# Second layer norm of a gated attention from the first one's variance, both inverse roots in one GpSimd operation

## The reference, cut to what matters

```python
def _layernorm(x, axis=-1, eps=1e-05):
    m, v = jnp.mean(x, axis=axis, keepdims=True), jnp.var(x, axis=axis, keepdims=True)
    return (x - m) / jnp.sqrt(v + eps)

x = x + _L0_ffn_ref(_layernorm(x), ...)        # sublayer 4: gate, top 2 of 8 experts, shared expert
x = x + _L1_attn_a_ref(_layernorm(x), ...)     # sublayer 5: the gated attention

def _L1_attn_a_ref(x, ...):                    # its x is already a layer norm
    residual = x
    mu, var = jnp.mean(x, -1, keepdims=True), jnp.var(x, -1, keepdims=True)
    xn = (x - mu) / jnp.sqrt(var + 1e-5) * gamma + beta
    ...                                        # q, k, v, alpha from xn; a scan over time
    return out + residual
```

## Time and profile before

| | us |
|---|---|
| runs (3) | 1042.56, 1044.42, 1044.64; median 1044.42 |
| the profiled execution, its own time | 1036.55 |
| its span, first to last instruction | 1034.8 |
| mean granted TensorE clock, share of full | 0.937 |

### The profile page before, as it was taken

The page is one execution under the profiler, slowest core; times in us unless marked ns, Lnnn a source line. Parts: engine busy times, 40 slices in busy tenths (PEclk is TensorE's granted clock), DMA queues, the critical chain, the costliest instruction groups (busy, mean ns, idle before and its releaser), DMA issues.

```text
span 1034.8 us, 16383 instructions
## 1 busy us (share of the span) xinstructions
PE 906.0 (88%) x5966; PEld 514.3 (50%) x5988; DVE 787.1 (76%) x1853; ACT 414.9 (40%) x686; POOL 369.4 (36%) x460
## 2 busy tenths in 40 slices
PE   8899999999999898879989875799999878988786
PEld 3344444444433465554434342565667456766454
DVE  5578888767788677788767679747666998788985
ACT  2445565554433354333534356123222334331233
POOL 6282333223343453422444320323021344343433
PEclk9899999999999988889999987899999899998889
DMA  5363122202000000000000000000000000000000
GB/s 130 97 177 103 48 69 62 73 1 108 0 1 1 1 2 1 1 1 2 0 1 1 1 0 2 2 1 1 1 2 1 1 1 1 2 1 3 1 10 31
DMA packets 11531, 24.32 MB, mean 24 GB/s; under 512 B 1323, under 2 KB 7635, under 8 KB 11315
## 3 DMA queue, kind: packets, MB, share of 16 engines
q1 hardware_dynamic: 11152, 22.30, 7.4%
q10 hardware_dynamic: 294, 0.91, 0.3%
HBM read 15.69 MB, written 7.34 MB: 22 GB/s over the span
## 4 chain that ended last, share of the span: by engine, by line
PE 57%; DVE 32%; issue 4%; POOL 3%; ACT 2%; DMA 0%; DVEq 0%; POOLq 0%; ACTq 0%
PE ps L1082 4%; PE ps L1075 4%; PE ps L1069 4%; PE ps L419 4%; PE ps L369 3%; DVE a_MN L549 2%; PE ps L2166 2%; DVE XN L166 2%; PE ps L389 2%; PE ps L2163 2%; DVE g_C L1922 2%; PE ps L2769 2%; DVE r_PP L2818 2%; PE ps L2177 1%; PE ps L1051 1%
## 5 line engine op out<-in xcount | busy, mean ns | idle before, releaser
L1322 POOL TENSOR_TENSOR f_Y<-f_Y,f_TT 128x512 f32<-128x512 f32 x54 | 69.9, 1294 | 126.9 <-DVE f_TT L1168 126.8
L549 DVE TENSOR_REDUCE a_MN<-ps 128x1 f32<-128x384 f32 (+3 forms) x154 | 93.1, 637 | 25.1 <-PE ps L372 23.4
L119 POOL TENSOR_TENSOR rs<-t,mhalf 128x4 f32<-128x4 f32 x36 | 37.4, 1038 | 131.5 <-DVE t L102 130.3
L673 ACT ACTIVATE a_PT<-ps 128x1024 f32<-128x1024 f32 x56 | 57.4, 1025 | 58.3 <-PE ps L389 58.1
L1082 PE MATMUL ps<-f_HH,pack_zero 128*128 128x512 f32 x128 | 67.7, 611 | 10.1 <-DVE f_TT L1168 10.1
L1268 ACT ACTIVATE f_HH<-ps,pack_zero 128x512 f32<-128x512 f32 x64 | 44.0, 687 | 71.1 <-PE ps L1069 71.1
L1069 PE MATMUL ps<-f_XS,pack_zero 128*128 128x512 f32 x128 | 67.6, 610 | 1.4 <-DVE f_XS L1037 0.9
L1075 PE MATMUL ps<-f_XS,pack_zero 128*128 128x512 f32 x128 | 68.7, 619 | 0.0
L1168 DVE SCALAR_TENSOR_TENSOR f_TT<-ps,pack_zero,f_X 128x512 f32<-128x512 f32 x64 | 47.7, 745 | 27.5 <-PE ps L1082 26.7
L369 PE MATMUL ps<-a_KS,a_QS 72*128 72x128 bf16 (+3 forms) x224 | 53.8, 303 | 8.2 <-DVE a_MN L549 7.2
L769 POOL TENSOR_SCALAR_AFFINE_SELECT a_PT<-a_PT 128x256 f32<-128x256 f32 x64 | 26.2, 413 | 87.8 <-ACT a_PT L673 87.2
(11 more groups left out here) (342 smaller groups left out, 2191.8 us busy)
## 6 DMA issues: line engine op xcount, KB each, us to landing
scratch<-a_parts SPq DMA_DIRECT2D x16, 384.0 KB, 3.3
a_QS<-scratch SPq DMA_DIRECT2D x14, 288.0 KB
a_KS<-scratch SPq DMA_DIRECT2D x42, 96.0 KB
pack_one<-in_one SPq DMA_DIRECT2D x1, 2694.5 KB, 9.5
pack_zero<-in_zero SPq DMA_DIRECT2D x3, 884.5 KB, 4.6
X<-in_x SPq DMA_DIRECT2D x4, 256.0 KB, 10.3
out_x<-X SPq DMA_DIRECT2D x4, 256.0 KB, 2.0
a_QS<-a_MT SPq DMA_DIRECT2D x42, 4.0 KB
```

The source lines that it names most:

```text
L549: dve.tensor_reduce(M.a_MN[:, n % 2, ti, h0:h0 + k], bank(M, M.bank["a_max", n, jj], 128 * (ti + 1) * k).rearrange("p (a c) -> p a c", a=k ...
L673: act.activation(M.a_PT[:, c % 8, 0:1024], M.ps[:, a * 512:a * 512 + 1024], ACT.Exp).then_inc(made.sem, made.tick(n, hh))
L1322: pool.tensor_tensor(M.f_Y[:, i, :], M.f_Y[:, i, :], M.f_TT[:, u % 3, :], ALU.add).then_inc(made.sem, made.tick(n, u))
```

## The change

The inner norm's statistics on XN are gone (4 `bn_stats`, 4 `bn_aggr`, one addition and one `pow` per batch, and their Newton step). Where DVE makes v + 1e-5 for the outer norm it now also makes v(1+1e-5) + 1e-10. The tiles rs, t1 and t2 get a second plane, and for n = 4 POOL's operations run on both planes (128x8 in place of 128x4). XM is scaled from X with the mean of the outer norm and the second root. That scaling stands at e = 6 (5 with `again`), where the statistics stood. The turns of batches 0 to 2 stand one iteration earlier on PE (16, 24, 31), which is ahead of the shared expert of that batch, and on DVE (17, 25, 32).

```diff
@@ norm_mean
-    dve.tensor_scalar(M.t1[:, a:z], M.mv[:, a:z, 1], 1e-5, None, ALU.add).then_inc(var.sem, var.tick(n, b))
+    if n == 4:
+        dve.tensor_scalar(M.t1[:, 1, a:z], M.mv[:, a:z, 1], 1.0 + 1e-5, 1e-10, ALU.mult, ALU.add).then_inc(var.sem, var.tick())
+    dve.tensor_scalar(M.t1[:, 0, a:z], M.mv[:, a:z, 1], 1e-5, None, ALU.add).then_inc(var.sem, var.tick(n, b))
+def roots(x, b, k):
+    return x[:, 0:k, 4 * b:4 * b + 4]
@@ norm_root
-    r, t, v = M.rs[:, a:z], M.t2[:, a:z], M.t1[:, a:z]
+    r, t, v = (roots(x, b, k) for x in (M.rs, M.t2, M.t1))      # k = 2 if n == 4 else 1
     pool.wait_ge(var.sem, var.at(n, b))
-    pool.tensor_tensor(r, v, M.mhalf[:, 0:4], ALU.pow).then_inc(root.sem, root.tick(n, b))
+    pool.tensor_tensor(r, v, M.mhalf[:, 0:4 * k].rearrange("p (k j) -> p k j", k=k), ALU.pow).then_inc(root.sem, root.tick(n, b))
@@ norm_refine (the Newton step on DVE, for the last batch)
-        newton(dve, S, M.t1[:, a:z], M.rs[:, a:z], M.t2[:, a:z])
+        newton(dve, S, roots(M.t1, b, k), roots(M.rs, b, k), roots(M.t2, b, k))
@@ norm_scale
-        dve.tensor_scalar(dst[:, t, :], src[:, t, :], M.mv[:, t, 0:1], M.rs[:, t:t + 1],
+        dve.tensor_scalar(dst[:, t, :], src[:, t, :], M.mv[:, t, 0:1], M.rs[:, k, t:t + 1],
@@ ffn_tensor
-        if n == 3 and u in (17, 25, 32):
-            b = (u - 10) // 8
+        if n == 3 and u in (16, 24, 31):
+            b = (u - 9) // 8
             turn_tensor(pe, S, M, 4, b, 7, M.XM, (S["normed"], (5, b)))
@@ ffn_vector
-        if n == 3 and u in (18, 26):
+        if n == 3 and u in (17, 25):
             turn_affine(dve, S, M, b - 2)
...
             elif e == (5 if again(u) else 6) and n == 3:
-                dve.wait_ge(S["normed"].sem, S["normed"].n)
-                norm_front(dve, S, M, 5, b - 1, M.XN)
-            elif e == (6 if again(u) else 7) and n == 3:
-                norm_back(dve, S, M, 5, b - 1, M.XN, M.XM)
+                norm_scale(dve, S, M, 5, b - 1, M.X, M.XM, k=1)
...
-        if n == 3 and u == 33:
+        if n == 3 and u == 32:
             turn_affine(dve, S, M, 2)
...
     if n == 3:
-        dve.wait_ge(S["normed"].sem, S["normed"].n)
-        norm_front(dve, S, M, 5, 3, M.XN)
-        norm_back(dve, S, M, 5, 3, M.XN, M.XM)
+        norm_scale(dve, S, M, 5, 3, M.X, M.XM, k=1)
@@ ffn_gpsimd
-        if b and n == 3 and e == (5 if again(u) else 6):
-            norm_root(pool, S, M, 5, b - 1)
...
-    if n == 3:
-        norm_root(pool, S, M, 5, 3)
```

More of the change, by code:

```diff
@@ L115, in norm_root @@
 def norm_root(pool, S, M, n, b):
-    var, root, a, z = S["variance"], S["root"], 4 * b, 4 * b + 4
-    r, t, v = M.rs[:, a:z], M.t2[:, a:z], M.t1[:, a:z]
+    var, root, k = S["variance"], S["root"], 2 if n == 4 else 1
+    r, t, v = (roots(x, b, k) for x in (M.rs, M.t2, M.t1))
     pool.wait_ge(var.sem, var.at(n, b))
-    pool.tensor_tensor(r, v, M.mhalf[:, 0:4], ALU.pow).then_inc(root.sem, root.tick(n, b))
+    pool.tensor_tensor(r, v, M.mhalf[:, 0:4 * k].rearrange("p (k j) -> p k j", k=k), ALU.pow).then_inc(root.sem, root.tick(n, b))
     if by_pool(n, b):
@@ L133, in norm_factors @@
     root, a, z = S["root"], 4 * b, 4 * b + 4
-    r, t, mean = M.rs[:, a:z], M.t2[:, a:z], M.mv[:, a:z, 0]
+    r, t, mean = M.rs[:, 0, a:z], M.t2[:, 0, a:z], M.mv[:, a:z, 0]
     pool.wait_ge(root.sem, root.n)
@@ L155, in norm_refine, with norm_scale @@
     root = S["root"]
-    a, z = 4 * b, 4 * b + 4
+    k = 2 if n == 4 else 1
     dve.wait_ge(root.sem, root.at(n, b))
     if not by_pool(n, b):
-        newton(dve, S, M.t1[:, a:z], M.rs[:, a:z], M.t2[:, a:z])
-def norm_scale(dve, S, M, n, b, src, dst, tiles=range(4)):
+        newton(dve, S, roots(M.t1, b, k), roots(M.rs, b, k), roots(M.t2, b, k))
+def norm_scale(dve, S, M, n, b, src, dst, tiles=range(4), k=0):
     normed = S["normed"]
@@ L703, in scaled @@
         for t in range(4 * b, 4 * b + 4):
-            act.activation(M.XN[:, t, :], M.X[:, t, :], ACT.Identity, bias=M.t2[:, t:t + 1], scale=M.rs[:, t:t + 1]).then_inc(made.sem, made.tick(b))
+            act.activation(M.XN[:, t, :], M.X[:, t, :], ACT.Identity, bias=M.t2[:, 0, t:t + 1], scale=M.rs[:, 0, t:t + 1]).then_inc(made.sem, made.tick(b))
     turn_scalar(act, S, M, 0, 0)
@@ L3132 @@
 BASE = {"X": ([128, NT, 128], F32), "XN": ([128, NT, 128], F32), "XNT": ([128, B * T], F32), "st": ([128, NT, 6], F32),
-        "mv": ([128, NT, 2], F32), "rs": ([128, NT], F32), "t1": ([128, NT], F32), "t2": ([128, NT], F32), "mhalf": ([128, 32], F32),
+        "mv": ([128, NT, 2], F32), "rs": ([128, 2, NT], F32), "t1": ([128, 2, NT], F32), "t2": ([128, 2, NT], F32), "mhalf": ([128, 32], F32),
         "f_B3": ([120, 8, 128], BF16)}
```

## The result

| | before | after |
|---|---|---|
| median of 4 runs, us | 1043.49 (1039.87 to 1044.64) | 1030.38 (1029.52 to 1034.27) |
| profiled execution, us | 1036.55 | 1029.52 |
| its span, us | 1034.8 | 1027.8 |
| first `up` of stage 3 to first wa matmul (L1871, after L1869), us | 138.7 | 130.2 |

The ratio of the runs is 0.9887 (95% interval 0.9851 to 0.9924): 11.8 us less, by the interval 7.9 to 15.5; the two medians of four are 13.1 apart. The forecast was 1034.0, 10.4 less than a median of 1044.4, with a range of 1031.2 to 1039.8. The median measured, 1030.38, is 0.8 under that range, but the median before came out lower too with its fourth run; the ratio times 1044.4 is 1032.6, inside it. For the profiled execution 1026.2 was forecast and 1029.52 measured. Lines after L102 are shifted in the changed kernel: L1082 is now L1089, L1168 is L1175, L166 is L173, L181 is L188, L1871 is L1869.

The account below looks back on a forecast made before the run. PE bounds the kernel, busy 906 of 1034.8 us, with DVE's inner norm making it wait. Gains of 4.0 + 3.0 + 3.4 = 10.4 us take the median from 1044.4 to 1034.0, range 1031.2 to 1039.8.

Parts of the forecast that it names:

- What there is to win: PE in the second feed-forward: 10.4 us idle waiting for DVE, plus 1.8 and 1.4 of slow clock, 13.6 in all.
- Part 1, the scaling's 2.0 us: DVE, each batch: XM's scaling takes 2.0 us beside a POOL addition, against 1.12 alone.
- Part 2, the new wait for turn_affine: PE's second shared matmul, iteration 17, batch 0 only: a new wait of 1.7 us, bounds 0 and 2.6.
- down(16)'s wait: PE in batch 0: down(16), now after the turn, still waits 0.3 us for DVE.
- Batch 0's clock: PE in batch 0: open whether the clock holds; if it falls, 1.8 us are not won, gain 2.2 not 4.0.
- The end: Batch 2: down(31) 0.35 us late, L1097 after 0.9 idle, clock held; gain 3.4 us, or 2.0 with low clock.
- The power: POOL's power on 8 elements takes 1.6 us, 0.6 more than now; covered, so cost nothing.
- Batch 3 is hidden: Batch 3's inner norm is hidden by 0.5 us behind twelve pairs of L1871; taking 4.5 us from it gives nothing.
- The sum: Second feed-forward: gains of 4.0 in batch 0, 3.0 in batch 1 and 3.4 in batch 2, 10.4 us.
- The profiled execution: The whole profiled execution goes from 1036.55 to 1026.2 us.
- The signs named beforehand: L1168's waits under 1.5 us, none for L1177, one L1054 wait of 1 to 2, L119 about 1.6, L1871 about 594.
- A: PE's waits move rather than go, 2.6 us at bank 7 in batch 0, low clock: gain 5.2, 1039.2 us; chance 22%.

Follow-up runs that it names:

- e11: Kernel before, with 14, 8 and 14 useless bf16 matmuls in PE's queue where it waits for DVE: 94.57 us memset to wa, against 97.45; ratio 0.9981.
- e3: Changed kernel with turns, affines and XM's scaling at later places, only statistics and second root gone: 88.60 us memset to wa, against 97.45 before; ratio 0.9914.
- e4: Changed kernel with XM's scaling one iteration later, early turns kept: 87.88 us memset to wa, against 89.0 for the changed kernel; ratio to before 0.9897.
- e5: Changed kernel with XM's scaling later in batches 0 and 1 only, turn_affine first in DVE's iterations 17 and 25: 85.64 us memset to wa; ratio to before 0.9882.
- e7: Changed kernel with each batch's two roots as two powers of 128x4 in place of one of 128x8: 89.00 us memset to wa; ratio to before 0.9912.
- e12: Changed kernel with an unused 128x32 power ahead of each of the four roots: 103.58 us memset to wa, against 89.0; one run, 1049.90 us.
- e6: Changed kernel with the last batch's inner norm given its own statistics and power again: 88.99 us memset to wa, against 89.0; ratio to before 0.9936.
- e2: Kernel before with only the turns and affines moved one iteration up, inner norm kept: 95.59 us memset to wa, against 97.45; ratio 0.9969.

## Why the prediction was right, and where it was off

The mechanism was right: the statistics and the root that are gone took most of PE's waits with them, and the low clock behind two of them. The size came out 2 us too large in the stage.

- *What there is to win*, 13.6 us: idle 10.4 and clock 3.2. Measured 13.3: the idle time is read off rows, and e11 puts the clock at 2.9 (3.2 was forecast). Right.
- *Part 1, the scaling's 2.0 us*: the one step that failed. I let it meet one addition in every batch. f_Z stands right behind f_Y at that iteration, the scaling met both and took 3.01, and PE waited 1.07 us for scale_tokens in each of two batches. e3 and e4 take the same work one iteration on: 2.42 us in batches 0 and 1 and no such wait. The shared interfaces of the Trainium skill's "GPSIMD Engine Reference", Specifications, agree with these rows (1.12, 2.06, 3.01 us). I counted one POOL operation too few, and the trace before had both signs: POOL's f_Z already stood 0.15 us behind f_Y at 528.38, and XM's scaling of batch 2 took 2.98 us (595.91).
- *Part 2, the new wait for turn_affine*: 1.7 us forecast, 1.41 measured, in batch 0 only. e4 still has it, and e5, which moves the affine ahead of the routing, doesn't; so its cause is the routing work ahead of the affine. Of down(16)'s wait, 0.3 forecast, nothing came.
- *Batch 0's clock*, left open: it held.
- *The end*: waits of 0.35 and 0.9 forecast, 0.50 and 0.76 measured; transposes 1.9, 2.02 measured.
- *The power*: 1.6 forecast, 1.65 measured (the rows from 1 to 4 elements give 0.13 us each, not the 0.14 written). In batch 2, 1.1 us of cover against 0.8 needed was forecast, so 0.3 left; 0.44 is left. It costs nothing, as forecast; e7 and e12 show how much that depends on its length.
- *Batch 3 is hidden*: right (e6, by the trace). The sentence behind it, on how late it would now be had it been left, had the size wrong (3.4 less the cover of 0.5, so some 3 us): DVE's residual and PE's L1869 both start from the end of L1107 and move together, and XM came 0.42 us late. In the trace before it was ready 0.28 us ahead of PE (614.46 and 614.74), and the first power is 0.64 us longer now.
- *The sum*: what stays was forecast at 0.3 + 1.7 + 0.35 + 0.9 = 3.25. Measured 1.07 + 1.41 + 1.07 + 0.50 + 0.76 = 4.8. 13.3 - 4.8 = 8.5, and the mark gives 8.45. The forecast of 10.4 was high by 2.1 of scale_tokens' waits, and the rest nearly cancels. The medians (13.1, 12.0 and 8.9 apart) scatter on both sides of 10.4. So the nearness of the medians to the forecast is in part luck: the first four runs gave more than forecast while the stage gave less, and what lies between isn't shown.
- *The profiled execution*: 1029.52, not 1026.2. Of the 3.3 us, 2.0 are the sum's; the mark of this execution stands 1.0 us later than before (507.98, 506.98), and its end from g_top on is 0.5 longer.
- *The signs named beforehand*: L1168's waits 0.5 us (under 1.5), none for L1177, one of 1.41 for the affine in batch 0, the power 1.65, and L1104 3.85 us behind the start of down(30) (3.7) all came. L1869 starts at 596.98 where 594 was forecast: 2.0 us by the sum and 1.0 by the later mark.
- *Rivals*: none came whole. A said that the waits move rather than go, for a gain of 5.2 us. Some did: of the 4.8 us that stay, 2.1 are at a place that nobody named. But batch 1 had no wait at bank 7 and the clock held (1.00 from 470 us to the end of the stage), and 8.45 were gained.

## What to carry to other kernels

Where PE waits for DVE, price the clock beside the idle time, as a cost that may come or not (e2), and look at what runs on PE behind the wait. When DVE work in SBUF is moved, look at every POOL operation that will run in its time, not only at the next one: the places and the order alone (e5) were worth 3.35 us here beside the 8.45 of the whole change. And compare versions by a mark inside the trace, since an execution's start scatters more than such a change gives.

## What the runs showed of the hardware

- The first 221.8 to 230.9 us of an execution (to the first `up` of stage 1) differ by up to 9 us between traces of kernels that are alike there, and stage 3's first 8 us by up to 1.5. The second is the clock, timeline of PE in the changed kernel and in e7, same instruction, same 0.87 us of idle time:

```profile
466.76 1.10 PE L1076 MATMUL ps<-f_XS,pack_zero 128*128 128x512 f32 x2 [0.87 <-DVE f_XS L1044]
```

```profile
467.18 2.04 PE L1077 MATMUL ps<-f_XS,pack_zero 128*128 128x512 f32 x2 [0.87 <-DVE f_XS L1045]
```

Between 468 and 470 us the granted clock is 1.00 in the first and 0.50 in the second.

- In one trace (e2) PE waited 2.64, 2.63 and 2.65 us at three places. The granted clock fell to 0.50 behind the second and stayed at 1.00 behind the other two.
- Four scalings of 128x128 on DVE took 1.12 us alone, 2.06 beside one POOL addition, 2.42 when they started inside one and met the next, and 3.01 when they met two in full. Single small operations took nearly the whole length of an addition (1.27 us in place of 0.19).
- POOL's power took 0.61, 1.01, 1.65 and 5.43 us on 1, 4, 8 and 32 elements per partition.
